# A tail of its own for the last block: pairs of tiles over eight PSUM banks, shorter Newton chains, and FFN statistics from the copied output

## Chip, cores and metric

One NeuronCore of a Trainium2 chip runs the whole program; the other cores are idle. The metric is the device time of one execution in microseconds (us), taken as the median over runs.

## The reference

The input x has two sequences of 2048 tokens with 1024 channels. The function is an attention layer and a routed low-rank FFN, each with a layer norm ahead of it and another behind it, and with a residual:

```
x = x + layernorm(attention(layernorm(x)))
x = x + layernorm(ffn(layernorm(x)))

attention: q = x @ wq (32 heads of 32), one k and one v of 32 channels for all heads,
           causal softmax(q k^T / sqrt(32)) v, then @ wo
ffn:       scores = 8 * softmax(x @ Wr^T + br)              (8 experts)
           out = 2 * sum over h of scores_h * (x @ A_h^T) @ B_h^T   (rank 16 each, 128 in all)
```

All data are float32.

## The kernel before, in words

**Blocks, units, slots.** The 4096 tokens are cut into 8 blocks of 512 (four tiles of 128); a sequence has four of them. A block's attention is done in 8 units of 4 heads, 64 units in all (n = 0 to 63). A unit of the q-th block of a sequence has 4(q+1) steps, one per 128 keys, and each step has one slot per head. A unit of a fourth block has 16 steps and 64 slots. For each slot TensorE (PE) forms the transposed scores in one of two banks (`scores`), ScalarE (ACT) takes the exponential into one of three `pr` buffers (`exps`), and PE multiplies a finished step with the values (`values`). Beside that PE forms the scores of the next unit the other way round in three banks, and VectorE (DVE) takes their row maxima (`maximum`). The softmax's denominator is a sum of `pr` over the steps: GpSimd (POOL) adds whole steps into `ds` (`add`), and PE at last multiplies `ds` with ones (`sum_keys`). The number `by_pe(n)` says how many of the last steps of a unit PE multiplies with ones itself, straight from `pr`, instead of POOL adding them: four in the third and fourth block of a sequence, none otherwise.

**What sets the order.** Each engine has its own program. All of them walk through units and slots, and a table, `pieces(engine, n)`, names the other work that is put behind a slot: times there are in 64ths of a unit. While a block is in attention, the block before it is finished (`post`): the product with wo (`proj`), the norm behind the attention and the residual (`att`), the norm ahead of the FFN, and the FFN (`lora`), tile by tile. All this goes through one shared PSUM bank, `PX`. In `lora` PE turns the tile (`lora_turn`), forms the 128 low-rank values and 8 logits (`lora_low`), turns the weighted values (`lora_slt`) and multiplies with B (`lora_up`), half a tile of 512 columns at a time. DVE takes the statistics of each half out of PSUM, then ACT copies the half to `zs`, and then PE may write the next half.

**The norms.** There is no square root: `rsqrt` makes 1/sqrt(variance + eps) on DVE from an integer guess and three Newton rounds, in 12 operations of one column each; each waits for the one before. In the block's interior they are dealt out in four parts.

**The last block.** It has no later block to hide behind. A part of its product with wo (6 of 8 inputs) is done early, in units 62 and 63, and kept in `t4` (`early_proj`, L1177). The rest is the tail: PE ends `values` and `sum_keys` of unit 63, DVE takes reciprocals and scales the attention's output a tile at a time (L792, L809), and then the four tiles go one after another through the same functions as before, in two banks for `proj` and one for all the rest, with two tile buffers `xr` and two `zs`. A tile's `xr` buffer is stored and then loaded with the tokens of the tile two further on.

The lines that the steps below touch, by the numbers of the profile: L531 and L528 `add`, L538 `mask`, L557 POOL's last addition, L603 `exps`, L609 the copy of a unit's output, L637 to L656 ACT's part of the FFN, L711 and L716 statistics, L737 to L754 `rsqrt`, L881 residual, L1053 `scores`, L1071 `values`, L1080 sums by PE, L1102 `sum_keys`, L1167 `proj`, L1190 to L1208 PE's part of the FFN.

## Time and profile before

| | us |
|---|---|
| median of 3 runs | 3691.83 |
| lowest and highest | 3685.55, 3704.39 |
| the profiled execution's own time | 3686.55 |
| its span, first to last instruction | 3684.8 |
| PE busy in it | 3314.1 |
| POOL, DVE, ACT busy | 2166.4, 2367.1, 1568.2 |

The span is the time between the first and the last instruction of one profiled execution; the rest of its own time, 1.75 us, lies around it. Busy times of engines overlap. Below, a row "`start us, us, engine line op out<-in xcount [idle before <-releaser]`" is one of the timeline: when the work began, how long it lasted, and for what the engine had been waiting. A float32 matmul stands in the trace as two passes, so x8 are four instructions. PEclk is the clock granted to TensorE: 1.00 is 2.4 GHz and 0.50 is 1.2 GHz.

### The profile page before, as it was taken

How to read it: one execution, taken by the hardware profiler on the slowest of the kernel's cores; microseconds unless marked ns; L12 is line 12 of the kernel's file. 1: busy time of each engine (PE TensorE's matmuls, PEld its weight loads, DVE VectorE, ACT ScalarE, POOL GpSimd, SP SyncE). 2: the span in 40 equal slices, each digit the busy share in tenths (PEclk: the TensorE clock that was granted, in tenths of full speed). 3: DMA queues.
4: the chain of work that ended last, by engine and by line, in shares of the span. 5: the costliest groups of instructions: out<-in, count | busy, mean ns of one | idle time of the engine just before them, and what ended most of it. 6: DMA issues, size and time to landing. Idle time of an engine off the chain costs nothing.

```text
span 3684.8 us, 45490 instructions
## 1 busy us (share of the span) xinstructions
PE 3314.1 (90%) x15704; PEld 1609.2 (44%) x15704; DVE 2367.1 (64%) x6548; ACT 1568.2 (43%) x3121; POOL 2166.4 (59%) x783
## 2 busy tenths in 40 slices
PE   5789998999999999998887999899999999998974
PEld 2344444444444444443344444444444444444432
DVE  3557776767767677763465667676776766666334
ACT  0333344444454444455322334444444554454531
POOL 0234666756665777768422366667576667777751
PEclk8999999999999999999998999999999999999996
DMA  3412111111111010010111211111110110000000
GB/s 80 125 47 73 35 44 35 58 35 32 30 32 52 21 32 27 21 32 19 58 52 41 73 41 45 34 38 50 40 33 27 30 29 27 27 21 21 13 0 35
DMA packets 132327, 144.05 MB, mean 39 GB/s; under 512 B 28024, under 2 KB 93560, under 8 KB 132096
## 3 DMA queue, kind: packets, MB, share of 16 engines
q1 hardware_dynamic: 132096, 141.13, 13.2%
q8 instruction: 125, 2.05, 0.2%
q14 instruction: 106, 0.87, 0.1%
HBM read 72.91 MB, written 16.78 MB: 24 GB/s over the span
## 4 chain that ended last, share of the span: by engine, by line
PE 57%; POOL 18%; DVE 13%; issue 5%; ACT 5%; SPq 2%; DMA 1%; POOLq 0%; ACTq 0%; DVEq 0%
POOL ds L531 13%; PE ps L1053 10%; PE ps L1071 10%; PE ps L1167 10%; PE ps L1027 8%; PE ps L1041 8%; DVE mx L776 4%; POOL ds L528 2%; ACT pr L603 2%; PE ps L1208 2%; PE ps L1102 2%; PE ps L1080 2%; SPq L434 2%; PE ps L1196 1%; DVE ps L792 1%
## 5 line engine op out<-in xcount | busy, mean ns | idle before, releaser
L603 ACT ACTIVATE pr<-ps 128x512 f32<-128x512 f32 (+3 forms) x2560 | 1303.6, 534 | 1538.8 <-PE ps L1053 1023.3
L531 POOL TENSOR_TENSOR ds<-ds,pr 128x2048 f32<-128x2048 f32 (+3 forms) x384 | 1557.9, 4057 | 241.3 <-ACT pr L603 217.5
L1053 PE MATMUL ps<-qs,ks 98*128 98x512 f32 (+3 forms) x2560 | 1369.8, 540 | 110.8 <-ACT pr L603 94.9
L776 DVE TENSOR_REDUCE mx<-ps 128x1 f32<-128x512 f32 x1536 | 996.0, 680 | 403.0 <-PE ps L1041 397.6
L1041 PE MATMUL ps<-ks,qs 96*128 96x512 f32 (+3 forms) x2560 | 967.3, 388 | 54.3 <-DMA qs<-q 28.1
L1053 PEld LDWEIGHTS ps<-qs,ks 98*128 98x128 f32 x2560 | 490.4, 192 | 807.3 <-ACT pr L603 513.3
L773 DVE CUSTOM_DVE_ANT_0 ps<-ps,mask_qk 128x128 f32<-128x128 f32 (+3 forms) x1024 | 489.0, 495 | 437.6 <-PE ps L1041 434.3
L1071 PE MATMUL ps<-pr,vs 128*32 128x512 f32 (+3 forms) x5120 | 617.4, 555 | 9.9 <-POOL pr L538 9.9
L1041 PEld LDWEIGHTS ps<-ks,qs 96*128 96x128 f32 x2560 | 497.2, 196 | 292.3 <-issue 135.5
L1027 PE MATMUL ps<-xT,wq_sb 128*128 128x512 f32 x1024 | 528.8, 617 | 13.7 <-DVE ks L846 10.3
L1167 PE MATMUL ps<-wo_sb,ao 128*128 128x512 f32 x928 | 479.3, 616 | 26.8 <-DVE q L765 25.1
L528 POOL TENSOR_TENSOR ds<-pr 128x2048 f32<-128x2048 f32 (+1 forms) x64 | 273.8, 4278 | 351.1 <-ACT pr L603 351.1
L538 POOL TENSOR_SCALAR_AFFINE_SELECT pr<-pr 128x512 f32<-128x512 f32 x192 | 122.1, 636 | 362.1 <-ACT pr L603 361.7
L792 DVE RECIPROCAL ps<-ps 128x128 f32<-128x128 f32 x256 | 244.4, 956 | 99.8 <-PE ps L1102 99.7
L1027 PEld LDWEIGHTS ps<-xT,wq_sb 128*128 128x128 f32 x1024 | 186.1, 194 | 179.6 <-issue 160.2
L1167 PEld LDWEIGHTS ps<-wo_sb,ao 128*128 128x128 f32 x928 | 168.5, 194 | 173.4 <-issue 129.4
L557 POOL TENSOR_TENSOR xr<-xr,zs 128x1024 f32<-128x1024 f32 x32 | 75.7, 2365 | 264.6 <-ACT zs L656 264.6
L1071 PEld LDWEIGHTS ps<-pr,vs 128*32 128x32 f32 x5120 | 101.7, 109 | 195.0 <-issue 160.6
L773 DVE DVE_READ_ACCUMULATOR2_ANT mx<- 128x1 f32 x1024 | 144.6, 141 | 0.0
L765 DVE TENSOR_TENSOR q<-ps,q 128x512 fp32r<-128x512 f32 x64 | 44.3, 692 | 134.6 <-ACT q L587 134.5
L527 POOL COPY ds<-pr 128x512 f32<-128x512 f32 x16 | 9.8, 610 | 180.2 <-ACT pr L603 180.2
L1208 PE MATMUL ps<-fb_sb,slT 128*128 128x512 f32 x128 | 81.1, 719 | 24.9 <-ACT zs L650 22.8
(124 smaller groups left out, 2037.9 us busy)
## 6 DMA issues: line engine op xcount, KB each, us to landing
qs<-q SPq DMA_DIRECT2D x768, 64.0 KB, 2.0
wq_sb<-in_L_attn_wq_dram SPq DMA_DIRECT2D x64, 512.0 KB, 4.3
t<-in_L_attn_x_dram SPq DMA_DIRECT2D x32, 512.0 KB, 6.6
xr<-in_L_attn_x_dram SPq DMA_DIRECT2D x32, 512.0 KB, 3.5
out_dram<-xr SPq DMA_DIRECT2D x32, 512.0 KB, 2.6
qs<-mT SPq DMA_DIRECT2D x256, 4.0 KB
wo_sb<-in_L_attn_wo_dram SPq DMA_DIRECT2D x1, 4096.0 KB, 13.9
zs<-in_L_ffn_A_dram SPq DMA_DIRECT2D x1, 512.0 KB
```

The costliest lines, as they stand in the source:

```text
L528: nc.gpsimd.tensor_tensor(ds[:, :, c0:], first[:, :, c0:], this, ALU.add).then_inc(added, 1)
L531: nc.gpsimd.tensor_tensor(ds[:, :, c0:], ds[:, :, c0:], this, ALU.add).then_inc(added, 1)
L603: nc.scalar.activation(pr[:, k % NS, g, c0:], ps[:, PST + head(n, t, g) % NPS, c0:], ACT.Exp, scale=SCALE).then_inc(exp_done, 1)
L773: nc.vector.tensor_tensor_reduce(out=seen, in0=seen, in1=mask_qk[:, BLK - w:], op0=ALU.add, op1=ALU.max, scale=1.0, scalar=3.0 * NEG, accu ...
L776: nc.vector.tensor_reduce(found, seen, AX.X, ALU.max).then_inc(mx_done, 1)
L792: nc.vector.reciprocal(part, part).then_inc(rden_ready, 1)
L1027: last = nc.tensor.matmul(ps[:, PX, :], wq_sb[:, n % NW, k, :], xT[:, k, :], start=(k == 0), stop=(k == KT - 1))
L1041: nc.tensor.matmul(ps[:, bank, 0:w], qs[0:STK, n % NS, g, qt * P:(qt + 1) * P], ks[0:STK, c:c + w], start=True, stop=True).then_inc(mx_rea ...
L1053: last = nc.tensor.matmul(ps[:, bank, c0:], ks[0:STK + 2, c:c + P], qs[0:STK + 2, n % NS, g, c0:], start=True, stop=not by_mask)
L1071: last = nc.tensor.matmul(ps[g * HD:(g + 1) * HD, PPV, c0:], vs[:, row, :], pr[:, (UNIT_STEP[n] + t) % NS, g, c0:], start=(t == 0), stop=( ...
L1167: last = nc.tensor.matmul(ps[:, proj_bank(j, h), :], ao[:, (n + k) % NAO, j % TB * P:(j % TB + 1) * P], wo_sb[:, k, h * HALF:(h + 1) * HAL ...
L1208: nc.tensor.matmul(ps[:, PX, :], slT[:, :], fb_sb[:, h * HALF:(h + 1) * HALF], start=True, stop=True).then_inc(y2_ready, 1)
```

## The change

Four things are changed.

1. `by_pe` is 6 instead of 4 in the last two units of each sequence's fourth block (units 30, 31, 62, 63).
2. `rsqrt` takes 8 operations instead of 12: eps and the factor 1/2 are applied in one, the shift is a product with -0.5 within the guess, and a guess of negative sign makes the last scaling unnecessary.
3. In `lora` the FFN's statistics are read from the copy in `zs`, no longer from PSUM; ACT copies as soon as PE is done. DVE's part and all behind it stand 2 or 4 64ths later in the table.
4. The last block's tail is written as a program of its own. Tile i has banks 2i and 2i+1. PE adds `t4` with a product with the identity (`tail_begin`), so DVE's additions go. Statistics and residual read PSUM. All tokens of the block are loaded to `xT` in unit 61. The Newton chains are run for two tiles at once, in 11 operations of two columns. Tiles go in pairs, (0, 1) and (2, 3). ACT makes the FFN's normed input. ACT scales the output straight from PSUM; the last addition is cut in halves, two of the eight on POOL and six on DVE, and so are the stores.

```diff
     def by_pe(n):
-        return TB if qb_of(n) >= 2 else 0
+        if qb_of(n) < 2:
+            return 0
+        return TB + 2 if qb_of(n) == 3 and n % NU >= 6 else TB
...
         for h in range(2):
-            for who in ("PE", "ACT", "DVE"):
+            for who in ("PE", "ACT"):
                 at(t0 + (up, up1)[h], who, "up", j, h)
+            at(t0 + (up, up1)[h] + later, "DVE", "up", j, h)
...
             def lora_up(j, h):
-                act.wait_ge(LN["ffn"]["s_st"], 2 * j + h + 1)
+                act.wait_ge(y2_ready, 2 * j + h + 1)
                 nc.scalar.copy(zs[:, j % 2, h * HALF:(h + 1) * HALF], ps[:, PX, :]).then_inc(y2_sb, 1)
...
-                chain(0, lambda: nc.vector.tensor_scalar_add(ve, L["mv"][:, i, 1:2], EPS))
-                chain(1, lambda: nc.vector.tensor_single_scalar(half, ve.bitcast(I32), 1, op=ALU.logical_shift_right))
-                for k in range(1, ROUNDS):
-                    chain(1, lambda: nc.vector.tensor_scalar_mul(L["c"][:, k, i:i + 1], ve, 0.25 ** k))
-                chain(2, lambda: nc.vector.tensor_scalar(y0, half, -1.0, float(MAGIC), ALU.mult, ALU.add))
+                chain(0, lambda: nc.vector.tensor_scalar(w, L["mv"][:, i, 1:2], EPS, 0.5, ALU.add, ALU.mult))
+                chain(1, lambda: nc.vector.tensor_scalar(y0, w.bitcast(I32), -0.5, float(MAGIC), ALU.mult, ALU.add))
...
             def lora_up(j, k):
                 if k < 2:
-                    dve.wait_ge(y2_ready, 2 * j + k + 1)
-                    stats("ffn", j, 0, k, ps[:, PX, :])
+                    dve.wait_ge(y2_sb, 2 * j + k + 1)
+                    stats("ffn", j, 0, k, zs[:, j % 2, k * HALF:(k + 1) * HALF])
...
+            def tail_begin(i, h):
...
+                nc.tensor.matmul(ps[:, tail_bank(i, h), :], ident[:, :], t4[:, i, h * HALF:(h + 1) * HALF], start=True, stop=False)
+                for k in range(EARLY, KT - 1):
+                    nc.tensor.matmul(ps[:, tail_bank(i, h), :], ao[:, (LAST * NU + k) % NAO, i * P:(i + 1) * P],
+                                     wo_sb[:, k, h * HALF:(h + 1) * HALF], start=False, stop=False)
...
             values(UN - 1, steps(UN - 1) - 1)
+            for i, h in HALVES[:3]:
+                tail_begin(i, h)
             sum_keys(UN - 1)
+            tail_begin(1, 1)
+            for i in range(TB):
+                tail_proj(i, 0)
+                if i == TB - 1:
+                    tail_begin(i, 1)
+                tail_proj(i, 1)
+                if i < 2:
+                    tail_begin(2 + i, 0)
+                if i == 0:
+                    tail_begin(2, 1)
+            for p in range(TB // 2):
+                pair = (2 * p, 2 * p + 1)
+                for i in pair:
+                    tail_turn(i, 0)
+                    tail_turn(i, 1)
+                for i in pair:
+                    tail_low(i)
+                for i in pair:
+                    tail_slt(i)
+                for i in pair:
+                    tail_up(i, 0)
+                    tail_up(i, 1)
```

DVE's program in the new tail, behind reciprocals and scaling:

```diff
+            tail_att(0)
+            tail_mid(0)
+            tail_att(1)
+            for p in range(2):
+                for i in (2 * p, 2 * p + 1):
+                    tail_logits(i)
+                if p:
+                    for i in (0, 1):
+                        tail_out(i, 0)
+                        tail_out(i, 1)
+                for i in (2 * p, 2 * p + 1):
+                    tail_weights(i)
+                if p == 0:
+                    tail_mid(1)
+                tail_ffn(p)
+            for i in (2, 3):
+                tail_out(i, 0)
+                tail_out(i, 1)
```

`tail_att` is the four statistics, the chain, two residuals and -mean*r; `tail_mid` the same without residuals, on `x4`; `tail_logits` adds the bias and takes the maximum of a tile, `tail_weights` the sum, reciprocal and weighting; `tail_ffn` is statistics, chain and shift; `tail_out` is the last addition where POOL does not do it. ACT's program in the new tail:

```diff
+            for p in range(TB // 2):
+                for i in (2 * p, 2 * p + 1):
+                    tail_norm(i, 0)
+                    tail_norm(i, 1)
+                    tail_turned(i, 0)
+                    tail_turned(i, 1)
+                if p:
+                    for i in (2 * p - 2, 2 * p - 1):
+                        tail_scale(i, 0)
+                        tail_scale(i, 1)
+                for i in (2 * p, 2 * p + 1):
+                    tail_exp(i)
+                for i in (2 * p, 2 * p + 1):
+                    tail_slT(i)
+            for i in (TB - 2, TB - 1):
+                tail_scale(i, 0)
+                tail_scale(i, 1)
```

**How instructions move, 1.** POOL's program through units 30 and 31, before (`ds` is the running sum, `pr` the exponentials, AFFINE_SELECT the mask):

```order
L528 TENSOR_TENSOR ds<-pr 128x2048
L531 TENSOR_TENSOR ds<-ds,pr 128x2048 x9
L538 AFFINE_SELECT pr<-pr 128x4x128
L531 TENSOR_TENSOR ds<-ds,pr 128x2048
L538 AFFINE_SELECT pr<-pr 128x4x128 x3
L528 TENSOR_TENSOR ds<-pr 128x2048
L531 TENSOR_TENSOR ds<-ds,pr 128x2048 x9
L538 AFFINE_SELECT pr<-pr 128x4x128
L531 TENSOR_TENSOR ds<-ds,pr 128x2048
L538 AFFINE_SELECT pr<-pr 128x4x128 x3
```

and now:

```order
L594 TENSOR_TENSOR ds<-pr 128x2048
L597 TENSOR_TENSOR ds<-ds,pr 128x2048 x8
L604 AFFINE_SELECT pr<-pr 128x4x128 x4
L594 TENSOR_TENSOR ds<-pr 128x2048
L597 TENSOR_TENSOR ds<-ds,pr 128x2048 x8
L604 AFFINE_SELECT pr<-pr 128x4x128 x4
```

Each of these units has two additions fewer, and the first mask no longer stands between two additions. PE has 4 matmuls `ps<-pr,ones 32x512` more for each of the two steps.

**How instructions move, 2.** PE's program from the end of unit 63, before:

```order
L1071 MATMUL ps<-pr,vs 32x128 x4
L1080 MATMUL ps<-pr,ones 32x128 x4
L1102 MATMUL ps<-ds,ones 32x512 x4
L1167 MATMUL ps<-wo_sb,ao 128x512 x8
L1190 MATMUL ps<-ident,zs 128x128 x8
L1196 MATMUL ps<-fa_sb,hT 128x136 x8
L1201 MATMUL ps<-ident,sl 128x128
L1208 MATMUL ps<-fb_sb,slT 128x512 x2
```

and now:

```order
L1250 MATMUL ps<-pr,vs 32x128 x4
L1259 MATMUL ps<-pr,ones 32x128 x4
L1446 MATMUL ps<-t,ident 128x512
L1448 MATMUL ps<-wo_sb,ao 128x512
L1446 MATMUL ps<-t,ident 128x512
L1448 MATMUL ps<-wo_sb,ao 128x512
L1446 MATMUL ps<-t,ident 128x512
L1448 MATMUL ps<-wo_sb,ao 128x512
L1281 MATMUL ps<-ds,ones 32x512 x4
L1446 MATMUL ps<-t,ident 128x512
L1448 MATMUL ps<-wo_sb,ao 128x512
L1454 MATMUL ps<-wo_sb,ao 128x512 x2
```

Six matmuls of 512 columns now stand ahead of the sum with ones (L1102, now L1281), on which the reciprocals depend.

**How instructions move, 3.** DVE's program at the FFN statistics of one tile of an interior block, before (ISA is the masked maximum):

```order
L773 ISA mx 128x1
L711 BN_STATS st_ffn<-ps 128x6
L773 ISA ps,mx<-ps,mask_qk 128x128
L773 ISA mx 128x1
L792 RECIPROCAL ps<-ps 128x128
L773 ISA ps,mx<-ps,mask_qk 128x256
L773 ISA mx 128x1
L711 BN_STATS st_ffn<-ps 128x6
L716 BN_AGGR mv_ffn<-st_ffn 128x2
```

and now:

```order
L885 RECIPROCAL ps<-ps 128x128
L866 ISA ps,mx<-ps,mask_qk 128x256
L866 ISA mx 128x1
L813 BN_STATS st_ffn<-zs 128x6
L866 ISA ps,mx<-ps,mask_qk 128x256
L866 ISA mx 128x1
L885 RECIPROCAL ps<-ps 128x128
L866 ISA ps,mx<-ps,mask_qk 128x256
L866 ISA mx 128x1
L813 BN_STATS st_ffn<-zs 128x6
L818 BN_AGGR mv_ffn<-st_ffn 128x2
```

The statistics read `zs` instead of PSUM, and stand behind more of the maxima than before.

## Rows read from the trace of the kernel before

**Rows 1.** The page's fourth part: the chain by engine and by line.

```profile
PE 57%; POOL 18%; DVE 13%; issue 5%; ACT 5%; SPq 2%; DMA 1%; POOLq 0%; ACTq 0%; DVEq 0%
```

**Rows 2.** Stretches: busy PE, PEld, DVE, ACT, POOL, then PEclk, DMA share, GB/s.

```profile
3496.70:3561.50 64.80, 58.73 (x285) 23.55 (x289) 4.09 (x5) 34.45 (x68) 52.43 (x15) 1.00 0.00 1
3545.10:3561.50 16.40, 12.84 (x92) 5.52 (x94) 0.00 (x0) 6.65 (x17) 11.47 (x6) 1.00 0.00 1
3478.10:3496.70 18.60, 15.89 (x99) 7.23 (x98) 0.00 (x0) 8.53 (x20) 11.48 (x6) 1.00 0.00 0
1698.90:1716.10 17.20, 13.61 (x94) 5.65 (x87) 1.97 (x8) 7.95 (x19) 11.52 (x6) 0.90 0.03 8
1763.60:1781.70 18.10, 14.08 (x92) 6.12 (x92) 3.68 (x14) 7.82 (x19) 11.48 (x6) 0.81 0.04 9
3561.40:3684.80 123.40, 55.19 (x164) 28.75 (x156) 67.74 (x236) 18.12 (x33) 9.39 (x4) 0.67 0.07 26
```

**Rows 3.** Timeline of POOL in unit 63.

```profile
3502.85 4.56 POOL L528 TENSOR_TENSOR ds<-pr 128x2048 f32<-128x2048 f32 x1 [8.20 <-ACT pr L603]
3507.55 42.06 POOL L531 TENSOR_TENSOR ds<-ds,pr 128x2048 f32<-128x2048 f32 x9
```

**Rows 4.** Timeline of the tail: TensorE, ScalarE, VectorE.

```profile
3561.40 1.04 PE L1102 MATMUL ps<-ds,ones 128*32 128x512 f32 x8
...
3563.71 0.96 DVE L792 RECIPROCAL ps<-ps 128x128 f32<-128x128 f32 x1
...
3564.91 0.96 DVE L792 RECIPROCAL ps<-ps 128x128 f32<-128x128 f32 x1
...
3568.58 0.19 PEld L1167 LDWEIGHTS ps<-wo_sb,ao 128*128 128x128 f32 x1 [0.24 <-issue]
...
3569.01 0.19 PEld L1167 LDWEIGHTS ps<-wo_sb,ao 128*128 128x128 f32 x1 [0.24 <-issue]
...
3572.81 1.28 DVE L881 SCALAR_TENSOR_TENSOR xr<-zs,r_att,xr 128x1024 f32<-128x1024 f32 x1
...
3575.70 0.15 DVE L744 TENSOR_SCALAR ve_mid<-mv_mid 128x1 f32<-128x1 f32 x1
...
3576.26 0.27 DVE L737 TENSOR_SCALAR a_mid<-y_mid,ve_mid 128x1 f32<-128x1 f32 x1
...
3578.12 0.81 DVE L895 TENSOR_SCALAR zs<-xr,mv_mid,r_mid 128x1024 f32<-128x1024 f32 x1
...
3578.99 1.11 PE L1190 MATMUL ps<-ident,zs 128*128 128x128 f32 x4 [7.24 <-DVE zs L895]
...
3582.63 3.59 PE L1196 MATMUL ps<-fa_sb,hT 128*128 128x136 f32 x16 [0.68 <-ACT hT L637]
...
3592.76 2.07 PE L1208 MATMUL ps<-fb_sb,slT 128*128 128x512 f32 x2 [0.37 <-ACT slT L646]
```

**Rows 5.** Timeline of the last tile's end: ScalarE.

```profile
3677.79 1.52 ACT L656 ACTIVATE zs<-zs,sh,r_ffn 128x512 f32<-128x512 f32 x2 [2.65 <-DVE sh L933]
```

**Rows 6.** Chain of the tail: start us, us, what; between the second and third tile.

```profile
3606.31 2.63 DMA out_dram<-xr
3608.95 3.46 DMA xr<-in_L_attn_x_dram
```

**Rows 7.** Groups of VectorE in the tail: count, busy us, mean ns, idle before.

```profile
L711 DVE BATCH_NORM_STATS2 st_ffn<-ps 128x6 f32<-128x512 f32 x8 | 5.6, 699 | 22.1 <-PE ps L1208 22.1
L711 DVE BATCH_NORM_STATS2 st_att<-zs 128x6 f32<-128x512 f32 x8 | 5.6, 694 | 0.3
L818 DVE TENSOR_TENSOR zs<-ps,t 128x512 f32<-128x512 f32 x8 | 5.4, 680 | 8.2 <-POOL xr L557 8.2
L912 DVE SCALAR_TENSOR_TENSOR sl<-ps,sm,le 128x128 f32<-128x128 f32 x4 | 1.4, 351 | 0.1
```

**Rows 8.** Waits up to 3562 us: us in total, times, longest.

```profile
ACT zs L650 <- DVE st_ffn L711: 97.4, 56, 4.1
...
PE ps L1208 <- ACT zs L650: 17.2, 20, 1.0
```

More of the change, by code:

```diff
@@ L217, in early @@
     def early(at):
+        at(64 * 5, "SP", "last")
         for i in range(TB):
@@ L362, in bass_mqa_sandwich_lora_router, with dve_outs @@
+        def dve_outs(i, h):
+            return sum(not by_pool(*x) for x in HALVES[:HALVES.index((i, h)) + 1])
+        HALVES = [(i, h) for i in range(TB) for h in range(2)]
         POOL_CONST = 7
```

313 lines of the change are left out of this document (221 added, 92 removed).

## The prediction

> **What bounds the kernel now.** I read the chain first [rows 1]: TensorE holds 57% of it, POOL 18%, VectorE 13%. No single engine bounds all of the span, so each part of the change must be priced in its own stretch. The stretches come next [rows 2]. The one to see is the last: from 3561.4 us, where unit 63's values end, to 3684.8 there are 123.4 us in which PE is busy for 55.2, DVE for 67.7 and ACT for 18.1, at a mean granted clock of 0.67. That is no full engine but four tiles handed from engine to engine, one after another. In between the chain even passes through a store of 2.63 us and a load of 3.46 us [rows 6], because the third tile needs the buffer of the first. In units 30, 31, 62 and 63 POOL's additions follow each other without a gap, ten from 3502.85 to 3549.6, 4.7 us each [rows 3]; POOL sets the pace there. But PE is busy for 58.7 of the 64.8 us of unit 63 [rows 2], so it is close behind. In the interior, the FFN's copies wait for the statistics [rows 8].
>
> **1. The tail.** I lay out the new program from t = 0 at the end of the values (3561.4 before), with the durations of [rows 4, 5, 7].
>
> *Up to the first pair's input.* Six matmuls now stand ahead of the sum with ones: 12 passes, each 0.43 behind the one before (the two weight loads of [rows 4]), so 5.2. The sum takes 1.04: t = 6.2. Nothing hides these 5.2 us; this is the part that the change makes worse. Four reciprocals with their scaling at 1.20 each: 11.0. Meanwhile PE needs 20 passes more until both halves of tile 1 are complete, 8.6: t = 14.8. DVE then lacks one statistic of tile 1 (0.70) and an aggregate (0.3): 15.8. The chain for two tiles has 11 operations. Before, 12 took 2.42 (from 3575.70 to 3578.12). No row shows an operation on two columns: the nearest are 0.15 (one column, L744) and 0.35 (128 columns, L912), plus some 0.04 to the next. I take 0.21, near the small one because the size is, so 2.3; the bounds are 2.1 and 4.3 if all were as slow as the large. t = 18.1. Two residuals at 1.28: 20.7; -mean*r 0.25: 21.0. Four statistics and two aggregates of the second norm 3.0, chain 2.3, shift 0.25: 26.6.
>
> *First pair, FFN.* ACT norms a half in 0.76 (half of the 1.52), PE turns it, ACT copies it in 0.59. By then PE has been idle for 5 us, so I use the slow durations: 1.11 for a half's four transposes, 3.59 for a tile's product with A. The two tiles are turned by 33.4 and the products end at 37.0 and, at half clock, 40.6. VectorE does the first norm of pair 2 from 26.6 to 35.2, beside this, at no cost; it is hidden as long as turning and product take longer than these 8.6 us. Logits, ACT's exponential, then 0.75 per tile for the weights: 42.6. Turning them and ACT's copy: 43.1. Four products with B at 1.75: 50.0.
>
> *Second pair.* DVE does its second norm from 42.6 to 48.1, beside those products. Norm, turns and copies, interleaved between ACT and PE, take about 8: 56. The products with A end at 59.6 and 63.2. DVE's logits 0.4, then two last additions of the first pair (0.68 each) that stand ahead of the weights: 65. Weights 1.5, turning and copy 0.7: 67. Products with B: 74. Last statistic and aggregate 1.0, chain 2.3, shifts 0.5: 77.8. ACT scales four halves at 0.76, DVE adds each behind it, 0.68 after the last: 81.6. The store of half a tile follows; a whole one took 2.63, I take 2.5: 84. POOL's two halves are done long before.
>
> The second product with A and the products with B may run at full clock, which would take up to 1.8 and 3.5 us away in a pair. The rows have the product with B at 2.07 for two passes at half clock (3592.76), and 0.43 per pass just after the last unit. I count one us of it: the new tail is **83**, a gain of 123.4 - 83 = **40**. The bounds: 79 with the second pair at full clock; 90 with slow operations of two columns (4 chains on the path, 1.9 more each) at half clock. So 33 to 44.
>
> Here the Trainium skill has a rule that speaks for the fast end ("TensorE: Matmul & The Clock Gate", Part 1): the clock is throttled by default and activity releases it. By it the four products with B, which now stand in a row, would run partly at 2.4 GHz and the tail would be nearer 79. No row shows four of them in a row, so this is not in the sum.
>
> Another rule speaks against the change. Statistics and residuals now read PSUM. The group of statistics from PSUM has 699 ns, that from `zs` 694 [rows 7], so I count nothing. The Trainium skill ("VectorE: DVE Perf Modes", section on the TRN2 errata) gives a fixed part of 58 cycles for SBUF and 120 for PSUM; an estimate from that page is 0.065 us for each of some 12 readings in the way, 0.8 us in all, and a gain of 39 in place of 40.
>
> **2. Two additions of each of four units go to PE.** POOL loses 8 x 4.7 = 37 us, but PE gets 8 times 1.04 (the price of the same four matmuls on `ds`, 3561.40). From the end of the ninth addition, at 3545.1, nothing is changed in what POOL allows; only behind it can the unit shrink. There 16.4 us pass, with PE busy for 12.84 [rows 2]; with 2.08 more it is 14.9, so at most 1.5 are to be had. By the same working 0.6 in unit 62 (18.6 against 15.89), 1.5 in unit 30 (17.2 against 13.61) and 1.9 in unit 31 (18.1 against 14.08), 5.5 in sum. With a busier PE the clock of 0.90 and 0.81 in the last two may rise. I take **6**. Bounds: 0 if masks and exponentials set the pace of the last steps, 16 if each whole unit shrank to its PE time (64.8 - 58.7 - 2.1 = 4 each).
>
> **3. FFN statistics from the copy.** In the interior ACT waited 97.4 us, over 56 halves, for the statistic before its copy, and 20 times PE stood idle for the second half, 17.2 us in all, 0.86 each [rows 8]. Taking one statistic (0.70 and 0.03) out of that way leaves 0.13: up to 14.6 us. (The 56 are 28 tiles of two halves, 8 of them in units of 64 slots, where PE is not idle at the second half but ACT's exponentials come late.) For those 8 tiles I take 0.7 a tile, 6 us. Of the sum of 20 not all stays, as POOL and DVE hold 31% of the chain: two thirds, **14**. Bounds: 0 and 25. What DVE now waits for comes later too, so the wait for PE that it had at these statistics is not worse unless the copy is late (rival C).
>
> **4. Shorter chains in the interior.** 12 operations took 2.42, of which 0.56 went by before the first Newton product at 3576.26. The same six products and roots and the last scaling make the other 1.86. Now there are two short ones at 0.19 ahead of the six, and no last scaling (0.19): 2.05. That is 0.37 less for each of 116 chains, 43 us of DVE. DVE holds 13% of the chain [rows 1], so **4** count; bounds 0 and 12. The time that DVE is beside PE hides the rest.
>
> The load of the last block's tokens moves to unit 61 on SP's queue, behind a wait for the last projection of queries, which PE has ended in unit 60. I cost it at nothing; if it did block, `rows` and `store` behind it would be late. What is late next in units 62 and 63 is PE itself.
>
> **Sum.** 40 + 6 + 14 + 4 = 64. From the profiled execution's own 3686.55 that gives 3622.5. That execution lies 5.3 below the median of the runs shown, so against the median 3691.83 - 64 = **3628 us**, the predicted time.
>
> **Rivals.**
> A. *Only the tail counts.* Parts 2 to 4 are hidden: in unit 62 PE is busy for 15.9 of 18.6 us at the end, and what PE gains from an earlier copy it then waits for elsewhere. For it speaks the 91% of busy PE in unit 63; against it that PE's idle time before the second half is measured. Time: 3692 - 40 = 3652, or 3648 with the clock.
> B. *Both go through in full.* Tail 44, units 16, FFN 25, chains 12: 97, so 3595. For it: 18% of the chain is POOL's. Against: PE's own busy time in these units.
> C. *A wait of DVE takes the place of ACT's, and it is slower.* In the interior DVE used to take the statistic as soon as PE was done. Now it must wait for ACT's copy, which stands in ACT's queue behind exponentials; behind DVE's wait stand the maxima, and PE has only three banks for their scores, so it would stop. To turn the forecast into a loss of over 0.5% (18 us) it would have to eat 64 + 18 us, 82 / 56 = 1.5 us of PE for each of the 56 halves. The copy takes 0.59 and the statistic is placed one or two slots later, so ACT would have to be some 2 us behind its slot each time. The order shows more maxima ahead of the statistic than before, which speaks against.
> D. *The tail does not shrink*, for example because every exchange between engines in the new order costs more than in the old, or PE's six matmuls before the sum push more than they save. It would need 40 us for that; with part of C, 3692 within 0.5%.
>
> **Chances.** Forecast 0.58, A 0.22, B 0.15, C 0.02, D 0.03. A difference of 0.5%, 18 us, is about what a measurement of this kernel can tell from no change. Faster by more than that: 0.95; within: 0.03; slower: 0.02. The range for 8 in 10 goes from 3604, towards B, to 3653, which takes in A: **3604 to 3653**.
>
> **What would show it.** In the new profile the span from the end of unit 63's values to the end should be 79 to 90 us. The sum with ones should come 5 us after the last values; the last reciprocal ends at t = 11; norms of pair 1 start at 27, of pair 2 at 48. A chain for two tiles should take 2.3. POOL should have nine additions in units 30, 31, 62, 63, each unit being 1 to 2 us shorter. ACT's wait before its FFN copy should fall from 97 us to under 50, and PE's before the second half from 17 to about 3. Wrong: a wait of DVE for the copy of over 1 us on average, a PE that waits for maxima there, or second-pair products that stand still while ACT scales the first pair.

## The result, and the profile after

The changed kernel takes 3581.97 us (median of 4 runs, 3579.33 to 3586.58) against 3692.04 us for the kernel before: a ratio of 0.970, 95% interval 0.9675 to 0.9725. It is 110 us faster. The forecast was 3628 us with a range of 3604 to 3653, so the direction was right and the gain was 1.7 times as large as forecast.

| | before | after |
|---|---|---|
| median, us | 3692.04 | 3581.97 |
| profiled execution's own time | 3686.55 | 3581.36 |
| its span | 3684.8 | 3579.6 |
| unit 63's output copied at | 3561.65 | 3505.37 |
| from there to the end | 123.2 | 74.2 |

The last two lines split the 105.2 us of the two spans: 56.3 lie ahead of the last copy and 48.9 behind it. The forecast had 24 and 40.

The page's chain after, by engine and line, answers to [rows 1]:

```profile
PE 57%; POOL 21%; DVE 10%; issue 5%; ACT 5%; SPq 2%; DMA 1%; POOLq 0%; ACTq 0%; DVEq 0%
```

VectorE went from 13% to 10%, POOL from 18% to 21%. The waits up to the last copy, after, answer to [rows 8]:

```profile
PE ps L1232 <- ACT pr L672: 67.0, 150, 3.0
...
ACT zs L719 <- PE ps L1382: 40.8, 48, 1.8
...
PE ps L1382 <- ACT zs L719: 2.2, 8, 0.3
```

and the first of them before:

```profile
PE ps L1053 <- ACT pr L603: 94.9, 148, 2.4
```

ACT's wait ahead of the FFN copies fell from 97.4 to 40.8 us and is now a wait for PE itself. PE's wait before the second half fell from 17.2 to 2.2, as forecast. But PE's wait for exponentials (94.9 us before, 67.0 after), which the forecast did not list, fell by 28 us, nearly twice as much as its wait before the second half. The stretches of the two traces say where. Columns are as in [rows 2]; first units 58 to 61 and 19 to 21 before, then after (a unit is counted from one copy of an output to the next):

```profile
3109.00:3430.10 321.10, 296.04 (x1441) 144.15 (x1442) 213.38 (x544) 155.67 (x304) 229.67 (x70) 0.95 0.08 23
881.40:1073.20 191.80, 183.07 (x940) 92.08 (x939) 136.58 (x376) 95.03 (x185) 121.55 (x44) 1.00 0.11 32
```

```profile
3068.10:3376.40 308.30, 289.25 (x1441) 140.57 (x1442) 209.47 (x504) 155.11 (x303) 229.59 (x70) 0.97 0.10 31
872.40:1060.80 188.40, 182.19 (x940) 92.36 (x941) 133.15 (x345) 94.75 (x185) 121.37 (x44) 1.00 0.11 33
```

The four units of 64 slots that hold an FFN lost 12.8 us with the same work on POOL (229.67 and 229.59 us). PE has the same 1441 instructions in both and is busy for 6.8 us less, at a granted clock of 0.97 instead of 0.95; the other 6.0 us are idle time of PE. The three units of 48 slots lost 3.4.

The new tail, in TensorE's and other engines' rows of the timeline, after:

```profile
3511.58 1.07 PE L1281 MATMUL ps<-ds,ones 128*32 128x512 f32 x8
...
3512.72 0.97 DVE L885 RECIPROCAL ps<-ps 128x128 f32<-128x128 f32 x1 [61.81 <-PE ps L1281]
...
3521.47 0.70 DVE L1070 BATCH_NORM_STATS2 ds<-ps 128x6 f32<-128x512 f32 x1 [0.16 <-PE ps L1454]
...
3522.44 0.17 DVE L1079 TENSOR_SCALAR ds<-ds 128x2 f32<-128x2 f32 x1
...
3524.61 2.48 DVE L1105 SCALAR_TENSOR_TENSOR xT<-ps,ds,xT 128x1024 f32<-128x1024 f32 x2
...
3532.45 1.52 ACT L768 ACTIVATE t<-xT,ds 128x512 f32<-128x512 f32 x2 [26.49 <-DVE ds L1098]
...
3538.43 5.33 PE L1467 MATMUL ps<-fa_sb,pr 128*128 128x136 f32 x32
...
3545.69 3.60 PE L1477 MATMUL ps<-fb_sb,ds 128*128 128x512 f32 x8
...
3550.71 1.52 ACT L768 ACTIVATE t<-xT,ds 128x512 f32<-128x512 f32 x2 [4.54 <-DVE ds L1098]
...
3556.65 4.77 PE L1467 MATMUL ps<-fa_sb,pr 128*128 128x136 f32 x32
...
3564.55 5.29 PE L1477 MATMUL ps<-fb_sb,ds 128*128 128x512 f32 x8
...
3573.49 2.78 ACT L786 ACTIVATE t<-ps,ds 128x512 f32<-128x512 f32 x4 [8.46 <-DVE ds L1148]
```

Counted from the end of the values at 3505.2, this gives the forecast's own milestones:

| | forecast, us | measured, us |
|---|---|---|
| sum with ones done | 6.2 | 7.4 |
| last statistic of the first norm, pair 1 | 15.5 | 17.0 |
| pair 1's FFN input can be normed | 26.6 | 27.2 |
| its products with A end | 40.6 | 38.5 |
| its products with B end | 50.0 | 44.1 |
| pair 2's input can be normed | 48.1 | 45.5 |
| its products with A end | 63.2 | 56.2 |
| its products with B end | 74.0 | 64.6 |
| shifts ready | 77.8 | 68.3 |
| end | 83 | 74.4 |

Up to pair 1's input the forecast holds to 1 us or so. Behind it lies the whole difference, most of it in PE's work. The granted clock (the column before the last two) for pair 1's turns, pair 1's products with A, pair 1's with B, pair 2's with A and with B:

```profile
3532.00:3539.00 7.00, 4.30 (x19) 3.90 (x20) 6.48 (x21) 5.01 (x8) 0.00 (x0) 0.50 0.00 1
3539.00:3544.00 5.00, 4.77 (x31) 4.57 (x29) 1.45 (x5) 0.56 (x2) 0.00 (x0) 0.76 0.00 0
3545.60:3549.20 3.60, 3.60 (x9) 1.43 (x9) 3.36 (x11) 0.28 (x1) 0.00 (x0) 1.00 0.00 0
...
3556.60:3561.40 4.80, 4.80 (x34) 4.62 (x32) 0.33 (x2) 3.48 (x7) 2.54 (x2) 0.80 0.14 55
3564.50:3569.90 5.40, 5.34 (x9) 1.97 (x9) 2.33 (x5) 0.28 (x1) 0.00 (x0) 0.68 0.15 60
```

Pair 1's four products with B ran at 2.4 GHz, 3.60 us and not the 7.0 of half clock; pair 2's ran at 0.68 and took 5.29. The two-column chain runs 2.17 us (3522.44 to 3524.61), 0.16 to 0.17 an operation and 0.20 from start to start, the small one of the two prices.

### The profile page after: what moved, and what is told of

The parts are those of the page before. It is cut to its first block, busy times and chain, and to the rows that moved or that the text cites. A ratio compares the mean times of both kernels' runs of the same rounds, so it can differ in the third digit from the quotient of the medians.

```text
span 3579.6 us, 45027 instructions
## 1 busy us (share of the span) xinstructions
PE 3306.6 (92%) x15784; PEld 1612.1 (45%) x15784; DVE 2299.5 (64%) x5996; ACT 1567.7 (44%) x3121; POOL 2121.2 (59%) x773
## 4 chain that ended last, share of the span: by engine, by line
PE 57%; POOL 21%; DVE 10%; issue 5%; ACT 5%; SPq 2%; DMA 1%; POOLq 0%; ACTq 0%; DVEq 0%
POOL ds L597 15%; PE ps L1232 10%; PE ps L1250 10%; PE ps L1341 9%; PE ps L1220 8%; PE ps L1206 8%; DVE mx L869 4%; POOL ds L594 3%; ACT pr L672 2%; PE ps L1259 2%; PE ps L1281 2%; SPq L493 1%; POOL xr L614 1%; PE ps L1370 1%; PE ps L1382 1%
## 5 line engine op out<-in xcount | busy, mean ns | idle before, releaser
L597 POOL TENSOR_TENSOR ds<-ds,pr 128x2048 f32<-128x2048 f32 (+1 forms) x376 | 1518.7, 4039 | 207.1 <-ACT pr L672 179.0
L1341 PE MATMUL ps<-wo_sb,ao 128*128 128x512 f32 x896 | 461.5, 613 | 24.1 <-DVE q L858 24.1
L1341 PEld LDWEIGHTS ps<-wo_sb,ao 128*128 128x128 f32 x896 | 161.0, 193 | 158.6 <-issue 119.4
L623 POOL TENSOR_TENSOR xr<-xr,zs 128x1024 f32<-128x1024 f32 x28 | 66.1, 2361 | 202.0 <-ACT zs L725 202.0
L1259 PE MATMUL ps<-pr,ones 128*32 128x512 f32 (+3 forms) x1088 | 103.6, 453 | 0.0
```

The source lines that it names most:

```text
L597: nc.gpsimd.tensor_tensor(ds[:, :, c0:], ds[:, :, c0:], this, ALU.add).then_inc(added, 1)
L1259: last = nc.tensor.matmul(ps[g * HD:(g + 1) * HD, PAUX, c0:], ones[:, :], pr[:, (UNIT_STEP[n] + t) % NS, g, c0:], start=(t == first), stop ...
L1341: last = nc.tensor.matmul(ps[:, PX, :], ao[:, (n + k) % NAO, j % TB * P:(j % TB + 1) * P], wo_sb[:, k, h * HALF:(h + 1) * HALF], start=(k ...
```

## The experiments

The end of a unit, that is ACT's copy of its output, comes at the same distance from the end of the unit before, to 0.05 us, in most units of most kernels. So the difference of two traces can be read unit by unit. In a few units it jumps by 1.3 to 3.8 us either way between executions, and the granted clock of the unit jumps with it: unit 47 took 40.27 us at PEclk 1.00 in the kernel before and in the changed kernel, 42.69 at 0.93 in `copy_alone`, and 42.6 at 0.87 in `sum_first` and `pair_first`. Kernels with the same program up to a unit differ by as much as 12 us in it (see `tail_alone`). Medians of parts are good to some 5 us for that reason, and I lean on the units. Where a kernel is compared with the changed kernel, the two medians are also of different sessions; the kernel before had 3692.0 to 3697.3 us in them.

### Each part alone

**The tail.** The changed kernel with the other three parts undone:

```diff
-        return TB + 2 if qb_of(n) == 3 and n % NU >= 6 else TB
+        return TB
...
-        h1, low, slt, up, up1, later = (4, 8, 16, 20, 24, 4) if N == 16 else (3, 6, 12, 14, 17, 2)
+        h1, low, slt, up, up1 = (4, 8, 16, 20, 24) if N == 16 else (3, 6, 12, 14, 17)
...
-                act.wait_ge(y2_ready, 2 * j + h + 1)
+                act.wait_ge(LN["ffn"]["s_st"], 2 * j + h + 1)
```

(and the 12-operation chains in the interior).

> The new tail on the interior of before (sums by POOL, 12 operations, statistics from PSUM in the interior). The whole change gave 110 us, of which the two traces show 49 behind the last values (123.4 before, 74.5 after) and 56 ahead of them. Theory: the two stretches are independent, so this kernel gives 46 to 52 us, and its units 0 to 63 end at the same times as before to within 1 us. Rival: the tail's length hangs on the clock that the last units leave behind; then it gives under 42 us.

It took 3645.7 us against 3693.05, a ratio of 0.989 (0.9852 to 0.9927): 47 us. From the last copy at 3573.43 to the end of its span of 3645.6 there are 72.2 us, 51.0 less than before. The stretch ahead of it was 11.8 longer than in the trace of before although the program there is the same but for a load; units 4, 5, 8, 27 to 29 and 35 to 43 make up most of it, in steps of 1.3 to 3.8 both ways (unit 5: 30.8 us at PEclk 0.93 before, 34.5 at 0.82 here). So the tail is worth 49 to 51 us by the traces, with the interior of before as with the changed one (the interval of the ratio is wider, 27 to 55 us); that the units end at the same times to 1 us was wrong, and each of the longer steps stands beside a lower granted clock in that unit.

**The FFN copy.** The kernel before with the copy ahead of the statistic and the shifted table:

```diff
-        h1, low, slt, up, up1 = (4, 8, 16, 20, 24) if N == 16 else (3, 6, 12, 14, 17)
+        h1, low, slt, up, up1, later = (4, 8, 16, 20, 24, 4) if N == 16 else (3, 6, 12, 14, 17, 2)
...
-                act.wait_ge(LN["ffn"]["s_st"], 2 * j + h + 1)
+                act.wait_ge(y2_ready, 2 * j + h + 1)
...
-                    dve.wait_ge(y2_ready, 2 * j + k + 1)
-                    stats("ffn", j, 0, k, ps[:, PX, :])
+                    dve.wait_ge(y2_sb, 2 * j + k + 1)
+                    stats("ffn", j, 0, k, zs[:, j % 2, k * HALF:(k + 1) * HALF])
```

(and `later` added to the slots of DVE's `up` and of all that follows it in `lora`).

> Only the FFN's copy ahead of its statistic, with DVE's part shifted in the table. Theory A: this is most of the 56 us of the interior, because ACT's exponentials no longer stand behind a wait for DVE: 28 to 40 us, with 1 to 2 us in each unit of 32 or 48 slots that holds an FFN and 2 to 5 in those of 64 slots. Rival B (the shorter chains did it): under 20 us. The forecast on record had 14.

3667.39 against 3693.05, ratio 0.9938 (0.9919 to 0.9957): 26 us. By units it shortened 26 to 29 by 3.2, 1.7, 3.3 and 4.2 us and 58 to 61 by 5.6, 1.7, 1.7 and 3.0, together 24.4; each of the eight units of 48 slots with an FFN (18 to 21, 50 to 53) by 0.9 to 1.0, together 7.7; others lost some of that in steps. The profiled execution is the slowest of its seven (3681.29 us). Theory A's amounts in the units are met, its total just missed.

**The short chains.**

The kernel before with chains of 8 operations, in the interior and in its own tail:

```diff
-                chain(0, lambda: nc.vector.tensor_scalar_add(ve, L["mv"][:, i, 1:2], EPS))
-                chain(1, lambda: nc.vector.tensor_single_scalar(half, ve.bitcast(I32), 1, op=ALU.logical_shift_right))
-                for k in range(1, ROUNDS):
-                    chain(1, lambda: nc.vector.tensor_scalar_mul(L["c"][:, k, i:i + 1], ve, 0.25 ** k))
-                chain(2, lambda: nc.vector.tensor_scalar(y0, half, -1.0, float(MAGIC), ALU.mult, ALU.add))
+                chain(0, lambda: nc.vector.tensor_scalar(w, L["mv"][:, i, 1:2], EPS, 0.5, ALU.add, ALU.mult))
+                chain(1, lambda: nc.vector.tensor_scalar(y0, w.bitcast(I32), -0.5, float(MAGIC), ALU.mult, ALU.add))
...
-                chain(done[0], lambda: nc.vector.tensor_scalar_mul(r, y, (-0.5) ** ROUNDS))
```

> Only the 8-operation chains, in the interior and in the old tail. There 12 chains are on the way, 0.37 us each: 4 us. Theory A: the interior gives 4 to 10 us more, so 8 to 14 in all. Rival B: DVE's 43 us less count nearly in full, since maxima stand behind the chains: over 25 us in all.

3682.01 against 3693.05, ratio 0.9967 (0.9948 to 0.9985): 11 us. The tail of this kernel is 3.0 us shorter. The interior gained 1.2 in each of units 9 to 11 and 41 to 43 and 0.9 in 12 and 44, all of 32 slots, and nearly nothing in units of 64 slots. Rival B, that DVE's 43 us count nearly in full, falls.

**The sums.**

The kernel before with two more sums on PE in units 30, 31, 62 and 63:

```diff
-        return TB if qb_of(n) >= 2 else 0
+        if qb_of(n) < 2:
+            return 0
+        return TB + 2 if qb_of(n) == 3 and n % NU >= 6 else TB
```

> Only the eight additions moved from POOL to PE. Forecast on record: 6 us (5.5 by busy time at the units' ends). The traces of before and after show 8.0 us for units 30 and 31 together, 2.6 for 62 and 63. Theory: 8 to 13 us, more in 30 and 31 because their granted clock rises from 0.81 to 0.90 towards 1. Rival: another part helped there, and alone it gives under 6.

3684.38 against 3693.05, ratio 0.9979 (0.9966 to 0.9992): 9 us. Units 30, 31 and 32 lost 3.7, 4.3 and 2.6 us, 62 and 63 1.3 and 1.7: 13.6 in sum, of which the median shows 9. The stretches of units 30, 31, 62 and 63 in the changed kernel answer to [rows 2, 3]:

```profile
1625.00:1686.50 61.50, 56.53 (x307) 23.67 (x306) 25.11 (x72) 34.16 (x67) 43.54 (x13) 1.00 0.09 22
1686.50:1747.90 61.40, 55.77 (x292) 21.75 (x291) 15.73 (x48) 34.38 (x68) 43.53 (x13) 0.97 0.09 23
3376.40:3441.70 65.30, 64.07 (x326) 27.86 (x326) 21.28 (x55) 35.67 (x69) 43.57 (x13) 1.00 0.00 1
3441.70:3505.30 63.60, 60.17 (x298) 24.19 (x298) 4.09 (x5) 34.54 (x68) 43.51 (x13) 0.99 0.00 1
```

PE is busy for 64.07 of 65.30 us in unit 62 and 60.17 of 63.60 in unit 63. Unit 62 was held by PE; in 63 PE still idles for 3.4 us. Over the whole of units 30 and 31 the granted clock rose from 0.95 and 0.92 to 1.00 and 0.97, and PE's busy time fell from 58.10 and 56.38 us to 56.53 and 55.71 although it has 16 passes more in each: the work that ran slow there shrank too. It does not in every execution. Unit 30 takes 63.0 to 63.2 us at 0.97 in `pair_first`, `sums_all` and `best`, which have the same six steps on PE, so 2.0 of its 3.7 us are there at either clock.

Four parts alone give 47 + 26 + 11 + 9 = 93 us of the 110. What the traces can say of the 17 is below.

### Is it ACT's wait?

`wait_back_64` takes the changed kernel and puts the old wait, the old source and the old place in the table back for the tiles whose FFN runs in units of 64 slots:

```diff
+        def by_psum(j):
+            return (j // TB + 1) % NQ == NQ - 1
...
             def lora_up(j, h):
-                act.wait_ge(y2_ready, 2 * j + h + 1)
+                if by_psum(j):
+                    act.wait_ge(LN["ffn"]["s_st"], 2 * j + h + 1)
+                else:
+                    act.wait_ge(y2_ready, 2 * j + h + 1)
```

> The changed kernel, but for the tiles whose FFN runs in units of 64 slots (26 to 29 and 58 to 61) ACT again waits for DVE's statistic, taken from PSUM at the old place; all else as changed. Alone, the copy gave 12.4 us in units 26 to 29 and 12.0 in 58 to 61, and about 1 us in each of eight units of 48 slots. Theory A (ACT's exponentials stood behind that wait, and with them the units of 64 slots): 22 to 27 us of the 110 are lost, in just those eight units. Rival B (the gain there belongs to the shift in the table, or to other parts together): under 12 us are lost.

3608.19 us, ratio 0.9758 (0.9724 to 0.9793) to before, 26 above the changed kernel. Units 26 to 29 lost 3.4, 1.9, 1.8 and 5.5 us, 58 to 61 3.4, 1.8, 3.4 and 3.0; 18 to 21 and 50 to 53 nothing over 0.04. Sixteen waits are worth 24 us, 1.5 each.

That is two effects of about the same size. With the same instructions, PE is busy for 10.2 us less in these eight units without the wait, because its granted clock is higher, and idle for 14.1 less. In `copy_alone` against the kernel before it is 11.7 and 12.6. Unit 58 before, in `newton_alone` (which has the wait) and in `copy_alone` (which has not):

```profile
3109.04:3193.89 84.85, 81.38 (x378) 40.09 (x379) 55.72 (x145) 39.51 (x77) 58.26 (x18) 0.94 0.10 29
```

```profile
3106.99:3188.03 81.04, 76.94 (x378) 38.31 (x379) 54.36 (x133) 39.52 (x78) 58.28 (x18) 1.00 0.10 30
```

```profile
3114.92:3194.17 79.25, 77.03 (x378) 38.23 (x379) 55.68 (x145) 39.45 (x78) 58.24 (x18) 1.00 0.11 31
```

At equal clock the copy is worth 1.8 us there, the clock 3.8. Units 27 and 59, at 1.00 with and without the wait, gained 1.7 and 1.6. The clock goes with the wait, though not strictly: unit 26 has 0.98 in the five kernels that have the old wait at its old place and 1.00 in all eight without it, unit 58 has 1.00 in all eight without and in one of the five with it.

`shift_alone` does the opposite: the kernel before with only the table shifted, so that ACT waits longer.

```diff
         for h in range(2):
-            for who in ("PE", "ACT", "DVE"):
+            for who in ("PE", "ACT"):
                 at(t0 + (up, up1)[h], who, "up", j, h)
+            at(t0 + (up, up1)[h] + later, "DVE", "up", j, h)
```

> The kernel before, with only the table's shift: DVE takes the FFN statistics 2 or 4 64ths later, still from PSUM, and ACT still waits for them before it copies. Theory A (ACT's wait is what costs): each of the 56 waits grows by one or two slots, so the kernel is slower than before by 30 to 90 us. Rival B (what helped is that DVE's maxima go first): same or faster than before.

3836.16 us, ratio 1.0375 (1.0339 to 1.0412): 142 us slower, outside what theory A had (30 to 90) and on its side; rival B is out. It is 2.5 us for each of 56 waits. ACT's wait for the statistic, 97.4 us before, is now

```profile
ACT zs L651 <- DVE st_ffn L712: 200.0, 56, 5.7
```

so 103 us more of waiting cost 142, and the granted clock fell too (1.00 to 0.93 in unit 18). The piece of the trace before that shows how a wait goes on through the engines, in unit 60:

```profile
3288.80 1.02 PE L1208 MATMUL ps<-fb_sb,slT 128*128 128x512 f32 x2
...
3290.65 0.68 DVE L711 BATCH_NORM_STATS2 st_ffn<-ps 128x6 f32<-128x512 f32 x1
...
3291.37 0.59 ACT L650 COPY zs<-ps 128x512 f32<-128x512 f32 x1 [2.01 <-DVE st_ffn L711]
...
3292.51 0.50 PE L1053 MATMUL ps<-qs,ks 98*128 98x512 f32 x1 [1.91 <-ACT pr L603]
3292.53 4.53 POOL L531 TENSOR_TENSOR ds<-ds,pr 128x2048 f32<-128x2048 f32 x1 [0.86 <-ACT pr L603]
```

PE had ended the half by 3289.8. DVE was at other work until 3290.65, ACT stood 2.01 us, the exponentials behind its copy came late, and PE with its two banks of scores stood 1.91 and POOL 0.86. POOL's idle time before its additions for exponentials, in the whole of units 58 to 61, before and after:

```profile
POOL ds L531 <- ACT pr L603: 13.6, 14, 3.2
```

```profile
POOL ds L597 <- ACT pr L672: 0.4, 1, 0.4
```

The 13.2 us that are gone match the 12.8 by which these units are shorter, and unit by unit they do so too: 6.2, 2.3, 2.3 and 2.9 us of POOL's idle time against gains of 5.7, 1.7, 2.4 and 3.0. (In unit 28 they do not, 0.8 against 3.4.) So ACT's wait broke POOL's row of additions. That POOL by itself set the pace is not shown: PE is busy for 77.0 of 79.2 us in units 58 and 59 of the changed kernel, and `sums_all` below takes two additions off POOL there without making them shorter. What is shown is that ACT's wait goes on to both.

### Rival C made stronger

`copy_no_shift` has the copy first but DVE's statistic at its old place, where ACT's copy is not ready.

```diff
             def lora_up(j, h):
-                act.wait_ge(LN["ffn"]["s_st"], 2 * j + h + 1)
+                act.wait_ge(y2_ready, 2 * j + h + 1)
...
-                    dve.wait_ge(y2_ready, 2 * j + k + 1)
-                    stats("ffn", j, 0, k, ps[:, PX, :])
+                    dve.wait_ge(y2_sb, 2 * j + k + 1)
+                    stats("ffn", j, 0, k, zs[:, j % 2, k * HALF:(k + 1) * HALF])
```

> The kernel before with the copy ahead of the statistic, but DVE's part left at its old place in the table. Rival C of the record, made stronger: DVE comes to the statistic while ACT has not yet copied, and the maxima behind it wait. Theory: DVE waits some 0.6 us (one copy) more than with the shift at each of 56 statistics; if that held up PE it would eat most of copy_alone's gain of 26 us. I expect half of it to be left, 10 to 20 us faster than before; rival: all of it, since PE has three banks of scores in hand.

3659.23 against 3696.34, ratio 0.9905 (0.9888 to 0.9921): 37 us, more than with the shift. By units, some 4 us of the difference belong to the shift (3.0 in units 26 to 29, 0.8 in 58 to 61, most of it at equal clock). The rest of what the two traces differ by up to the last copy, 21 us in all, lies in units such as 13, 15, 22, 38 and 47 (9.5 us together), whose granted clock is lower in `copy_alone`. VectorE's group of statistics, without the shift:

```profile
L711 DVE BATCH_NORM_STATS2 st_ffn<-zs 128x6 f32<-128x512 f32 x56 | 38.7, 691 | 37.4 <-ACT zs L650 37.4
```

and with it:

```profile
L712 DVE BATCH_NORM_STATS2 st_ffn<-zs 128x6 f32<-128x512 f32 x56 | 38.6, 689 | 0.0
```

DVE waits 37.4 us for the copies, 0.67 each, and it costs nothing that shows: the maxima behind it were not urgent. My expectation (half the gain eaten) was wrong. Units 26 to 29 even gained 3.8, 2.3, 3.6 and 5.8, more than with the shift.

### The start of the tail

The prediction called the six matmuls ahead of the sum "the part that the change makes worse". `sum_first` moves the sum ahead of them:

```diff
             values(UN - 1, steps(UN - 1) - 1)
+            sum_keys(UN - 1)
             for i, h in HALVES[:3]:
                 tail_begin(i, h)
-            sum_keys(UN - 1)
             tail_begin(1, 1)
```

> The changed kernel with the sum with ones ahead of the three pairs of matmuls that the record called the part that nothing hides (5.2 us). Forecast on record: the tail gets 5 us shorter. Theory from the trace after: PE works without a gap from the last values to the last product of tile 1 (3505.3 to 3521.5), so the order of its work there changes nothing: within 0.5 us in the tail, though the first reciprocal comes 6 us earlier.

The first reciprocal came 1.7 us after the last copy, in the changed kernel 7.3. The tail behind that copy was 73.99 us, in the changed kernel 74.23 (median 3585.58, ratio 0.9698, 0.9665 to 0.9732; its interior was 6.5 us longer). The same tail took between 72.2 and 74.8 us in `tail_alone`, `sums_all`, `sums_three`, the changed kernel and `wait_back_64`, at a granted clock of 1.00 to 0.92 over its first 17 us, so 0.2 us is within that; inside the tail the last statistic of pair 1's first norm came 0.4 us earlier, though the reciprocals came 5.6 earlier. DVE only waits: its statistic in `sum_first` shows

```profile
3521.64 0.70 DVE L1070 BATCH_NORM_STATS2 ds<-ps 128x6 f32<-128x512 f32 x1 [3.14 <-PE ps L1454]
```

and the changed kernel's PE is busy for 17.00 us of these 17:

```profile
3505.00:3522.00 17.00, 17.00 (x50) 7.09 (x43) 7.39 (x13) 0.58 (x1) 0.00 (x0) 0.93 0.00 1
```

`pair_first` does what follows from that: after the sum only pair 1's begins and products, then pair 2's.

```diff
-            for i in range(TB):
+            for i in (0, 1):
                 tail_proj(i, 0)
-                if i == TB - 1:
-                    tail_begin(i, 1)
                 tail_proj(i, 1)
-                if i < 2:
-                    tail_begin(2 + i, 0)
-                if i == 0:
-                    tail_begin(2, 1)
+            for h in range(2):
+                tail_begin(2, h)
+            tail_begin(3, 0)
...
```

> The changed kernel with the sum first and then only the work of the first pair, before any of the second: 16 passes of begin and 8 of proj after the sum instead of 32 in all ahead of tile 1's end. If PE's stream is what bounds the start, the first pair's last product ends 3.4 us earlier by the two begins that no longer stand ahead (8 passes at 0.43), and the tail is 3 to 3.5 us shorter. Rival: the reciprocals or the clock bound it, under 1 us.

The tail was 70.53 us, 3.7 shorter than the changed kernel's and below all five of the same tail. Its row for the last statistic of pair 1's first norm,

```profile
3523.41 0.70 DVE L1070 BATCH_NORM_STATS2 ds<-ps 128x6 f32<-128x512 f32 x1 [0.16 <-PE ps L1454]
```

lies 12.3 us behind its last copy at 3511.07, against 16.1 in the changed kernel (3521.47 from 3505.37) and 15.7 in `sum_first`: 3.4 us between the two that differ in this order alone, as expected. The median, 3581.41 (ratio 0.9684, 0.9643 to 0.9724), hides it behind 5.7 us of clock in the interior.

### More sums on PE

`sums_all` makes it six steps in all sixteen units of 64 slots, `sums_three` seven in units 30, 31, 62 and 63.

```diff
-        return TB + 2 if qb_of(n) == 3 and n % NU >= 6 else TB
+        return TB + 2 if qb_of(n) == 3 else TB
```

> The changed kernel with PE summing six steps in all sixteen units of 64 slots, not in four. PE gets 2.08 us more in each of twelve units, POOL loses 9.4 there. Theory: in units 24 to 29 and 56 to 61 PE is the bound, so each gets up to 2 us longer: 10 to 25 us slower than the changed kernel. Rival: POOL's additions set the pace there too (they hold 15% of the chain), then each gets 1 to 4 us shorter: 12 to 48 us faster.

3583.42 (0.9704, 0.9687 to 0.9721), as the changed kernel. Neither side held for all units: 24 and 56 got 1.7 longer, 25 to 27 and 57 to 59 0.6 to 1.0, but 28, 60 and 61 got 1.6, 4.6 and 2.2 shorter. (`sum_first`, `pair_first` and `sums_three`, with nothing changed there, also have 60 and 61 0.6 to 0.8 shorter.) So PE holds most of these units and POOL's additions hold 28, 60 and 61.

```diff
-        return TB + 2 if qb_of(n) == 3 and n % NU >= 6 else TB
+        return TB + 3 if qb_of(n) == 3 and n % NU >= 6 else TB
```

> The changed kernel with PE summing seven steps in units 30, 31, 62, 63 instead of six. Theory: the first additions moved gave 3.7, 4.3, 1.3 and 1.7 us in these units; what is left of POOL's lead is small in 62 and 63, so one more step gives 0 to 1 us there and 0 to 2 in 30 and 31, 0 to 4 in all, and it begins to cost PE's 1.04 each where PE is the bound.

3588.94 (0.9716, 0.9702 to 0.9731): units 30 and 31 1.6 longer each, 62 0.9 longer, 63 0.4 shorter. Units 30 and 31 have PEclk 1.00 here, so the clock is not the reason. Two steps more are the right number of those tried; the expected gain of 0 to 4 was not there.

### The two finds together

`best` is `pair_first` with the table's shift undone:

```diff
-        h1, low, slt, up, up1, later = (4, 8, 16, 20, 24, 4) if N == 16 else (3, 6, 12, 14, 17, 2)
+        h1, low, slt, up, up1 = (4, 8, 16, 20, 24) if N == 16 else (3, 6, 12, 14, 17)
...
-            for who in ("PE", "ACT"):
+            for who in ("PE", "ACT", "DVE"):
                 at(t0 + (up, up1)[h], who, "up", j, h)
-            at(t0 + (up, up1)[h] + later, "DVE", "up", j, h)
```

> The changed kernel with the tail's first pair first, and with the table's shift undone (copy ahead of the statistic, DVE's part at its old place). From the traces: pair_first's tail is 3.7 us shorter than the changed kernel's; without the shift the copy gave 0.6, 0.6, 0.3, 1.6 us more in units 26 to 29 and 0.6, 0.6, 0, -0.3 in 58 to 61, about 3.5 us. So a tail of 70 to 71 us and 7 us in all: about 3575 us, below both kernels. Rival: the two gains are within what the clock does to the interior, and the median is as the changed kernel's, 3582.

It took 3573.49 us (5 runs, 3566.97 to 3575.44), ratio 0.9658 (0.964 to 0.9676) to the kernel before and 8.5 us under the changed kernel's 3581.97; the slowest of its runs is below the fastest of the changed kernel. By the trace, 3.8 us of that are the tail (70.4 us) and 2.7 the units with an FFN, against an expected 3.7 and 3.5.

## Why the prediction was wrong

**The tail (step 1): right in mechanism, 9 us short.** The forecast had 83, 79 at best, and it is 74.4. What was mis-sized are TensorE's stages on the way, priced with rows at half clock. Pair 1's products with A took 5.3 us where 7.2 were put, pair 2's 4.8 where 7.2 were put, and pair 2's products with B 5.3 where 7.0 were put: 6 us, of which the text took off one ("I count one us of it"). Turning took 6.0 and 5.9 us in place of 6.8 and 7.9, 3 us more; the small stages between give the rest. Pair 1's products with B were furthest off, 3.6 for 6.9, but that counted for nothing: they stand beside DVE's second norm of pair 2, which ends later (45.5 against 44.1), and the forecast too went on from that norm, at 48.1. The bound of 79 granted full clock to the second pair alone, where the first one already had more of it than the second (1.00 and 0.68 over the products with B). In the trace PE was busy for 4.30 of 7.00 us at a granted clock of 0.50 while pair 1 was turned, then for 4.77 of 5.00 at 0.76, and then had 1.00; before, with single tiles, the tail had 0.67 on the whole, and now 0.80. The Trainium skill ("TensorE: Matmul & The Clock Gate", Part 1) was the better guide here; by its rule that activity releases the clock the forecast had put the tail near 79, and the measured 1.00 over pair 1's products with B agrees with it; the 0.68 over pair 2's, with PE busy for 5.34 of 5.40 us, agrees only in part. The chains of two columns took 2.17 us, near the lower bound of 2.1.

**"Nothing hides these 5.2 us" was wrong.** PE's work for pair 1 hid them: PE is the bound from the last values to 3521.5, and moving the sum in front changed the tail by 0.2 us, less than executions of the same tail differ by. What did cost there is the work for pair 2 that stands among that of pair 1, 3.7 us.

**The sums (step 2): 6 forecast, 13.6 in the units of the trace, 9 in the median.** The working by PE's busy time at the units' ends gave 0.6 and 1.5 for units 62 and 63, and 1.3 and 1.7 came (1.3 and 1.3 in the changed kernel). For 30 and 31 it gave 1.5 and 1.9, and 3.7 and 4.3 came, with 2.6 more in unit 32. The busy time taken there was measured at a granted clock of 0.90 and 0.81; the text said that the clock may rise and left it out of the sum.

**The FFN copy (step 3): this is the step that failed.** 14 were forecast, 26 came with the shift, 37 without. Of the 20 places where PE stood idle for the second half, the eight in units of 48 slots were priced well: these units got 0.9 to 1.0 us shorter, where the forecast's full amount was 0.73 each. The twelve in shorter units gave 0.75 or less, or went under in steps of the clock. But the 16 halves in units of 64 slots were "0.7 a tile, 6 us", and they are worth 24 us, 3 a tile, by two experiments that agree (24.4 put in, 24.3 taken back): about 1.7 a tile at equal clock, and the other half because the granted clock is higher without the wait (0.94 and 1.00 in unit 58). The forecast took the statistic's own 0.7 us out of the way; but ACT stood 2.6 us a copy in these units (41.6 us for the sixteen), because DVE came late to the statistic, and the exponentials behind the copy were as late. PE is not idle at the second half there, so the row on which the forecast priced the copy said nothing; the price was in PE's wait for exponentials, 94.9 us, and in POOL's broken row of additions. The factor of two thirds then took a third off. The upper bound of 25 was too low for the same reason.

**The chains (step 4): 4 forecast in the interior, about 9 by the units** of 32 slots, and 3.0 in the old tail. DVE's share of the whole chain, 13%, was used as if it held everywhere. In units of 32 slots nearly all counts, in those of 64 nearly nothing.

**The rivals.** A (only the tail) is out: all three other parts gave something. B (all in full, 3595) was nearest, and even it was 13 too slow. C is out, also in its stronger form: a wait of 0.67 us of DVE at each statistic cost nothing that shows. D is out. The range let B's 97 us stand outside; with B's own errors of size, it should have reached below it.

**What stays open.** The four parts alone sum to 93 us by their medians and together give 110. The interval of the tail alone reaches from 27 to 55 us, so the 17 us are hardly clear of noise. Ten of them lie in units 5, 13, 22 and 47, where the profiled `copy_alone` is 1.6 to 3.9 us longer than the changed kernel, at a granted clock of 0.82, 0.90, 0.97 and 0.93 against 0.93, 0.94, 1.00 and 1.00. Both have the shift of the table, `tail_alone` (unit 5) and `newton_alone` (unit 22) show the same losses without it, and unit 47 has the loss in `sum_first` and not in the changed kernel, with the same program up to there. So these are steps of the clock and not the shift; for unit 13 no other kernel settles it. Why the clock takes such a step in one execution and not in another is not known.

## What to carry to other kernels

Price a wait by what stands behind it in the queue of the engine that waits, not by the idle time of the engine one looks at: in the units of 64 slots ACT's 2.6 us at a copy cost nothing at the copy and 1.5 us further on, where PE and POOL came to wait for the exponentials behind it, half of it in idle time and half in clock. When several engines are within a few per cent of each other, a share of the chain over the whole span is no factor for a local gain; read each kind of stretch. And where work is merged into longer runs, work out TensorE's part at both clocks that the rows show, not only at the one that the old order had, and let the range span both.

## What was not expected of the hardware

The same program's units differ between executions by steps of about 1.5 to 3.8 us, and the granted clock of the unit steps with them. The kernel before ranged over 3681 to 3702 us in 22 runs and over 3684 to 3716 in 7 others; the changed kernel over 3579 to 3587 in 4, where the four of before beside it had 3686 to 3704. So single medians of small parts carry an error, and unit times are to be compared at equal clock. Statistics of 512 columns took 0.689 us from `zs` and 0.696 from PSUM in the interior, and the residual of 1024 columns 1.281 from PSUM in the new tail against 1.284 from SBUF in the old. Reading PSUM cost next to nothing. By the figures of the Trainium skill ("VectorE: DVE Perf Modes", section on the TRN2 errata) it would be dearer by 0.065 us each time, an estimate; here the measurement decides against it for these two operations.
